# A two-normalisation, three-layer channel network on 16 images: one GELU over both token halves of the lower channels, shorter GroupNorm chains, and another instruction order

## What is computed

```python
x = x + had(gn(x))                      # gn: 32 groups of 6 channels; had: 192 x 192 Hadamard block
h = gn(x)                               # x: (16, 192, 56, 56)
h = gelu(layernorm(W1 h + b1) * g1 + beta1)     # over the 192 channels of each pixel
h = gelu(layernorm(W2 h + b2) * g2 + beta2)
x = x + W3 h + b3
```

## Time and profile before

| | us |
|---|---|
| median of 3 runs | 1047.11 |
| lowest and highest | 1045.45, 1048.05 |
| the profiled execution | 1043.52 |
| its span, first to last instruction | 1041.7 |

### The profile page before, as it was taken

The page is one execution under the profiler, slowest core; times in us unless marked ns, Lnnn a source line. Parts: engine busy times, 40 slices in busy tenths (PEclk is TensorE's granted clock), DMA queues, the critical chain, the costliest instruction groups (busy, mean ns, idle before and its releaser), DMA issues.

```text
span 1041.7 us, 25024 instructions
## 1 busy us (share of the span) xinstructions
PE 932.8 (90%) x9384; PEld 638.9 (61%) x9384; DVE 868.4 (83%) x1553; ACT 890.1 (85%) x2821; POOL 612.5 (59%) x477
## 2 busy tenths in 40 slices
PE   0637898999998999999998999999999999999995
PEld 0216565666666666666765666666676666677662
DVE  6798999998999899999899989999889877854542
ACT  0727887899988998899988998889998999899992
POOL 0533654566665667556665667566665666666662
PEclk9967999999999999999999999999999999999997
DMA  9524021132222222222322232222101111011111
GB/s 288 158 78 109 28 81 55 54 107 77 85 81 81 81 81 86 77 85 78 107 71 74 85 94 81 81 81 81 54 31 52 34 50 54 28 54 55 54 46 62
DMA packets 49080, 80.66 MB, mean 77 GB/s; under 512 B 5568, under 2 KB 48704, under 8 KB 48832
## 3 DMA queue, kind: packets, MB, share of 16 engines
q1 hardware_dynamic: 48960, 79.06, 24.8%
HBM read 40.51 MB, written 38.54 MB: 76 GB/s over the span
## 4 chain that ended last, share of the span: by engine, by line
PE 68%; DVE 22%; POOL 3%; ACT 2%; issue 2%; SPq 1%; DMA 1%; POOLq 0%; ACTq 0%; DVEq 0%
PE tm L415 18%; PE tp L427 9%; PE tm L409 8%; PE tm L402 5%; PE hl L351 5%; PE hl L315 4%; DVE z L871 3%; PE hl L373 3%; PE tp L433 3%; PE hl L356 3%; PE hl L368 3%; DVE X L745 3%; DVE bn L720 3%; DVE x_lo L861 2%; PE hl L320 2%; DVE xs_lo L736 2%
## 5 line engine op out<-in xcount | busy, mean ns | idle before, releaser
L626 POOL TENSOR_TENSOR ge_lo<-ge,ge_hi 128x672 f16<-128x672 f32 x224 | 334.5, 1494 | 131.4 <-ACT ge_hi L532 131.4
L617 POOL TENSOR_TENSOR rs<-ssq,neg_half 112x4 f32<-112x4 f32 x224 | 246.6, 1101 | 228.0 <-ACT z L503 228.0
L503 ACT ACTIVATE z<-tm 112x194 f32<-112x194 f32 x896 | 284.3, 340 | 29.0 <-PE tm L415 29.0
L871 DVE TENSOR_TENSOR z<-tm,rs 112x768 f32<-112x768 f32 x224 | 212.6, 949 | 55.7 <-POOL rs L617 54.2
L516 ACT ACTIVATE ge<-tp,par 128x448 f32<-128x448 f32 x224 | 163.6, 731 | 53.6 <-PE tp L427 45.6
L503 ACT ACTIVATION_READ_ACCUMULATOR z<-tm 112x1 f32 x896 | 194.9, 217 | 0.0
L532 ACT ACTIVATE ge_hi<-ge 128x672 f16<-128x672 f32 x224 | 174.4, 778 | 2.2
L427 PE MATMUL tp<-cst,z 112*128 112x112 f32 x896 | 134.9, 273 | 14.8 <-DVE z L871 13.0
L745 DVE SCALAR_TENSOR_TENSOR X<-hl,h_bias,X 128x448 f32<-128x448 f32 x161 | 105.0, 678 | 50.4 <-PE hl L320 42.3
L427 PEld LDWEIGHTS tp<-cst,z 112*128 112x128 f32 x896 | 89.5, 142 | 87.8 <-issue 59.6
L494 ACT ACTIVATE x_hi<-X,gscale 128x448 f16<-128x448 f32 x168 | 106.8, 671 | 21.2 <-DVE gscale L819 21.2
(11 more groups left out here) (138 smaller groups left out, 2181.5 us busy)
## 6 DMA issues: line engine op xcount, KB each, us to landing
X<-x SPq DMA_DIRECT2D x56, 448.0 KB, 3.7
out<-X SPq DMA_DIRECT2D x56, 448.0 KB, 2.7
X<-x SPq DMA_DIRECT2D x112, 112.0 KB, 3.7
out<-X SPq DMA_DIRECT2D x112, 112.0 KB, 2.8
X<-weights SPq DMA_DIRECT2D x1, 1024.0 KB, 12.2
cst<-consts SPq DMA_DIRECT2D x1, 704.0 KB, 9.7
X<-biases SPq DMA_DIRECT2D x1, 192.0 KB, 2.5
par<-params SPq DMA_DIRECT2D x1, 6.5 KB, 1.6
```

Source lines behind the costliest of these rows:

```text
L503: last = nc.scalar.activation(z[n][:, 2 * h + k, i * TW:(i + 1) * TW], tm[h][:, i, k * TW:(k + 1) * TW], ACT.Square, scale=float(C) ** -0. ...
L617: nc.gpsimd.tensor_tensor(rs[n][:, 2 * h:2 * h + 2, :], ssq[n][:, 2 * h:2 * h + 2, :], neg_half[0:TT, 0:4].rearrange("p (i k) -> p i k", i=2),
L626: nc.gpsimd.tensor_tensor(ge_lo[n][:, g % 2, :, cols], ge[n][:, :, cols], ge_hi[n][:, g % 2, :, cols], ALU.subtract).then_inc(s_ge_lo[n], 1)
L871: nc.vector.tensor_tensor(z[n][:, 2 * h:2 * h + 2, 0:2 * C].rearrange("p k (i o) -> p i k o", i=2), tm[h][:, :, 0:2 * TW].rearrange("p i ( ...
```

## The change

One: `gelu` of the lower channels. Both halves' transposes of the lower channels now go into the two halves of `tp`'s bank 1, and one ACT instruction of 448 columns, in the call for h = 1, takes both. The tiles `ge`, `ge_hi`, `ge_lo` are laid out anew: [upper h0 image 0, image 1, upper h1 image 0, image 1, lower h0, lower h1], each 224 columns; `gelu_hi` and `gelu_lo` take parts of 448 (h = 0) and 896 columns (h = 1) instead of 672 and 672. `group(g, 1, 0)` waits for both parts. The matmuls keep their number and sizes.

Two: small operations. `gn_shift` leaves out the factor -1 and writes both copies with one instruction (the sign moves to `gn_h_bias` and `gn_w1_bias`, which subtract); `gn_w1_bias` works on 128 partitions in three instructions instead of ten on 2-row slices; `layer_biases` likewise. In the prologue fewer `stats_x` blocks stand between the parts of the second GroupNorm (7 instead of 10, the rest goes to step 0), `gn_w1_bias(0)` stands before `x1_split_lo(0, b)`, and on POOL `groupnorm_rstd(0, 1)` stands behind the subtraction for `w3_lo`.

Three: the order of the calls in `step` on PE, ACT, DVE and POOL.

```diff
-FIRST_STATS = {0: (42, 42), 1: (42, 52), 2: (52, 56), 3: (56, 63)}
+FIRST_STATS = {0: (42, 42), 1: (42, 54), 2: (54, 54), 3: (54, 63)}
...
-                    pe.wait_ge(s_ge_lo[0], 2 * g + h + 1)
+                    pe.wait_ge(s_ge_lo[0], 2 * (g + 1))
...
             def step(g):
                 group(g, 0, 0)
+                transposes(g - 2, 1, 1)
                 h_ab(h_unit(g, 0))
-                transposes(g - 2, 1, 1)
                 group(g, 0, 1)
                 h_c(h_unit(g, 0))
                 gn_means(gn2_pair(g), 1)
+                group(g - 1, 1, 0)
                 gn_means(gn1_pair(g), 0)
                 transposes(g, 0, 0)
-                group(g - 1, 1, 0)
                 l3_ab(g - 2)
                 transposes(g, 0, 1)
+                group(g - 1, 1, 1)
                 w1_shift(gn2_pair(g))
-                group(g - 1, 1, 1)
...
-                nc.scalar.activation(ge[n][:, 2, cols], tp[:, 1, 0:HALF], ACT.Gelu,
-                                     bias=par[:, 4 * n + 3:4 * n + 4], scale=par[:, 4 * n + 1:4 * n + 2]).then_inc(s_ge[n], 1)
+                if h == 1:
+                    act.wait_ge(s_tp[n], 3 * (g + 1))
+                    nc.scalar.activation(ge[n][:, 4:6, :], tp[:, 1, 0:2 * HALF].rearrange("p (b t) -> p b t", b=2),
+                                         ACT.Gelu, bias=par[:, 4 * n + 3:4 * n + 4], scale=par[:, 4 * n + 1:4 * n + 2]
+                                         ).then_inc(s_ge[n], 1)
...
-            groupnorm_rstd(0, 1)
             pool.wait_ge(s_whi, 3)
             nc.gpsimd.tensor_tensor(w3_lo[:, :, :], w3st, w3_hi[:, :, :], ALU.subtract).then_inc(s_wlo, 1)
+            groupnorm_rstd(0, 1)
...
-                for rows in two:
-                    last = nc.vector.tensor_copy(bias_rows[0][rows, 0, 0:C], b_row[rows, :])
-                do(last)
-                for rows in two:
-                    last = nc.vector.scalar_tensor_tensor(out=b_row[rows, :], in0=bias_rows[0][rows, 0, 0:C],
-                                                          scalar=row1[rows, :], in1=b_row[rows, :],
-                                                          op0=ALU.mult, op1=ALU.subtract)
+                do(nc.vector.tensor_copy(b_hi[:, :], b_row[:, :]))
+                nc.vector.scalar_tensor_tensor(out=bias_rows[0][:, :, 0:C],
+                                               in0=b_hi[:, :].unsqueeze(1).to_broadcast([128, 2, C]), scalar=low_row,
+                                               in1=b_row[:, :].unsqueeze(1).to_broadcast([128, 2, C]),
+                                               op0=ALU.mult, op1=ALU.add).then_inc(s_bias, 1)
```

More of the change, by code:

```diff
@@ L27 @@
 BND = 6
+PART = (slice(0, 2), slice(2, 6))
 AA, CA_, AC_, CCB, CCD = range(5)
@@ L350, in l3_ab @@
                     for r, (w, act) in enumerate(terms):
-                        nc.tensor.matmul(hl[:, i, 0:UT], w[:, AA, :], act[:, i, :], start=(r == 0), stop=False,
+                        nc.tensor.matmul(dst[:, i], w[:, AA, :], act[:, i:4:2, :], start=(r == 0), stop=False,
                                          skip_group_check=True)
@@ L355, in l3_ab @@
                         rows = slice(64 * i, 64 * i + 64)
-                        last = nc.tensor.matmul(hl[:, i, 0:UT], w[rows, CA_, :], act[rows, 2, :], start=False,
+                        last = nc.tensor.matmul(dst[:, i], w[rows, CA_, :], act[rows, 4:6, :], start=False,
                                                 stop=(r == 2), skip_group_check=True)
@@ L367, in l3_c @@
                 for r, (w, act) in enumerate(terms):
-                    nc.tensor.matmul(hl[:, 0, 0:UT], w[:, CCB, :], act[:, 2, :], start=(r == 0), stop=False,
+                    nc.tensor.matmul(dst, w[:, CCB, :], act[:, 4:6, :], start=(r == 0), stop=False,
                                      skip_group_check=True)
@@ L372, in l3_c @@
                         cols = slice(64 * i, 64 * i + 64)
-                        last = nc.tensor.matmul(hl[cols, 0, 0:UT], w[:, AC_, cols], act[:, i, :], start=False,
+                        last = nc.tensor.matmul(dst[cols], w[:, AC_, cols], act[:, i:4:2, :], start=False,
                                                 stop=(r == 2), skip_group_check=True)
@@ L422, in transposes @@
                 pe.wait_ge(s_z[n], 2 * g + h + 1)
-                done = 4 * g + 2 * h
+                done = 3 * g + h
                 free("tp0")
@@ L729, in first_stats @@
                 if g == 0:
-                    stats_x(range(31, 42))
+                    stats_x(range(28, 42))
             def scaled_lo(a, b):
@@ L807, in gn_shift @@
                     return
[L808 removed]
                 dve.wait_ge(s_grs, gn_use(q, n) + 1)
                 scale = (gscale1[:, q % 2, :], gscale2[:, :])[n]
[L811 to L818 removed]
+                for rows, cols, w in ((slice(0, 128), slice(0, 2), 2), (lower[0], slice(2, 3), 1), (lower[1], slice(3, 4), 1)):
+                    if n == 0:
+                        nc.vector.tensor_tensor(gshift[0][rows, cols, 0], gmu[rows, 0, cols], scale[rows, cols], ALU.mult)
+                    else:
+                        shape = [rows.stop - rows.start, w, 2]
+                        nc.vector.scalar_tensor_tensor(out=gshift[1][rows, cols, :],
+                                                       in0=gmu[rows, 0, cols].unsqueeze(2).to_broadcast(shape),
+                                                       scalar=b3[rows, cols.start:cols.start + 1],
+                                                       in1=scale[rows, cols].unsqueeze(2).to_broadcast(shape),
+                                                       op0=ALU.add, op1=ALU.mult)
                 nc.vector.tensor_copy(scale[lower[1], 2:3], scale[lower[1], 3:4]).then_inc(s_gn[n], 1)
```

161 lines of the change are left out of this document (73 added, 88 removed).

## The result

The changed kernel takes 998.68 us (median of four runs, 997.27 to 999.54) against 1047.58 us of the kernel before on the same chip (four runs): a ratio of 0.9536, 95% interval 0.9516 to 0.9555. The profiled execution took 999.41 us, its span is 997.6 us; the span before was 1041.7.

The account below looks back on a forecast made before the run. It took PE, busy without a gap, to bound regular steps at 15.8 us. Terms -4.0 (prologue), -6.0 (steps 0 to 5), -18.5 (GroupNorm), -2.5 (end), +1.3 (tail) sum to -29.7: median 1047.1 to about 1017, range 1008 to 1037.

Parts of the forecast that it names:

- The two tight waits: Regular step: `group(g-1, 1, 0)` waits for `z(g, 0, 0)`, half a microsecond left, and for all of `ge_lo`, 4.7 us left.
- rivals A: Regular step: the half microsecond before layer 2's first half is eaten, 0.4 us in each of 42 steps, 1034; chance 0.15.
- D: Regular step: `ge_lo` holds DVE instructions 1.7 us beyond DVE's slack, 42 times, so slower, 1088; chance 0.10.
- The idle times of 1.49, 1.05 and 1.20: GroupNorm steps: PE's waits at `w1_shift`, the next `h_ab` (six steps each) and `l3_c` (four) go, 20.0 us together.
- the 1.5 kept back for ACT: GroupNorm steps: 20.0 cut to 18.5, as ACT's wait in `split_x1(g+1, 0)` can make transposes 0.2 to 0.4 late.
- 0.3 is left: GroupNorm steps: the bias ends at 17.1 us from the step's start, the next step starts at 17.4.
- it passes: GroupNorm steps: the last bias instruction starts 0.2 us behind an `rs` whose successor isn't ready, so it isn't held.
- Rival B: GroupNorm steps: bias caught behind `rs` and the 896-column `ge_lo`, 2.3 us in each of six steps, 1031; chance 0.10.
- All these read two operands from SBUF: DVE and POOL: such DVE instructions are held when `ge_lo` runs or waits behind `rs`, for the rest of both.
- the prologue's 4.0: Prologue gain: 1.1 stuck operation, 1.7 for three `stats_x`, 1.8 shorter bias, less 0.6 waiting for PE's means.
- I get 1.8 gained over steps 0 and 1: Steps 0 and 1: three blocks return (1.7), but `normalise` precedes the statistics and `GELU` isn't behind `scaled_hi`; 1.8 us gained.
- Rival C: Norm steps: DVE is next, PE's gaps reappear ahead of other blocks; only prologue and removed instructions count, 1030; chance 0.07.

Follow-up runs that it names:

- `h_ab` turned round: Kernel after, with the 64-row matmuls of `h_ab` first and those over 128 rows and 96 columns after them; 1008.7 us, ratio 0.9636.
- before, with one piece of PE's order: Kernel before, with `transposes(g-2, 1, 1)` moved ahead of `h_ab(h_unit(g, 0))` on PE, nothing else; 1080.86 us, ratio 1.0331.
- transposes ahead of `l3_c`: Kernel after, with `transposes(g - 1, 1, 0)` moved ahead of `l3_c(g - 2)` on PE; 1023.28 us, ratio 0.9773.

## Why the prediction was wrong, point by point

**The regular step, where it failed.** "PE bounds such a step without a gap; a step can't be shorter unless PE's work shrinks, and the change leaves every matmul as it is", and then "So I expect 15.8 again". I had set PE's blocks one behind the other with lengths taken beside their old neighbours, and a block's length belongs to the pair. Over five kernels, in regular steps without idle time (PE busy for all of each window):

| kernel | shape changes between blocks | regular step, us |
|---|---|---|
| before | 8 | 15.78 |
| `h_ab` turned round | 7 | 15.59 |
| before, with one piece of PE's order (step 47) | 6 | 15.50 |
| after | 5 | 15.35 |
| transposes ahead of `l3_c` | 4 | 15.20 |

Counted from the kernel after, each change is worth 0.12 to 0.15 us. Three of them, 0.43 a step, in 42 steps are 18 of the 21 us by which steps 6 to 47 beat the forecast. The trace of before could have told it: in its `l3_ab` matmuls of 448 columns start 0.19 us apart, and the 64-row pair behind them 0.29 after the last. `l3_ab` waits only at its head, so this tenth can't be a wait:

```profile
606.91 0.35 PE L351 MATMUL hl<-ge_lo,w_hi 128*128 128x448 f16 x1
607.10 0.35 PE L351 MATMUL hl<-ge_hi,w_lo 128*128 128x448 f16 x1
607.39 0.36 PE L356 MATMUL hl<-ge_hi,w_hi 64*128 64x448 f16 x2
```
The Trainium skill (TensorEngine Tiling (Array Packing), Key Properties) says that changing the tiling mode drains TensorE. The trace agrees, and puts 0.12 to 0.15 us to one change; I had not weighed that rule, though the change consists of moved blocks.

**The two tight waits of the regular step.** Right: no idle time in it, rivals A and D did not occur. The runs with only a part of the orders show how narrow it was, 0.2 to 1.4 us of waiting in each regular step.

**The GELU.** "I cost it at nothing by itself": in the regular step it measured 0.06 us, close. "It pays only where ACT was late": it does pay outside the regular steps, and I put no number to that. With the new orders the part is worth 13.8 us in all. That ACT is what is late there isn't shown; in step 27 of the run without it PE waits 0.54 us for a residual of DVE.

**GroupNorm steps.** Of 20.0 gross I took 18.5; 21.4 came. The idle times of 1.49, 1.05 and 1.20 are all gone, and the 1.5 kept back for ACT wasn't needed. (The 21.4 rest on taking 0.43 for each of the 42 steps.)

**The bias.** "0.3 is left" and "it passes" were right, by less than 0.2 us. Rival B was real in its mechanism and forecast too cheap: 2.3 us in each of six steps, where the run with the old small operations lost 6.5 in each of seven. I had left out that the clock is low behind a gap of 4 us. And "All these read two operands from SBUF" was too narrow: the cast was held too. The Trainium skill (SBUF — State Buffer, Who interferes with whom) counts casts and copies that go into a mode with two ports among those that exclude GpSimd; the 2.58 us of the cast agree. `x_lo` at 563.39 isn't alone: all eight `x_lo` of the kernel before that began inside an `rs` took 0.68 or 0.69, and the last bias operation of the kernel after took 0.62 wholly inside the `rs` from 535.55, as it does with no `rs` about (71.31). An `rs` alone held none of them. Why the `gshift` triple at 522.37, with a `ge_lo` right behind the `rs`, was held and `x_lo`, with one right behind as well, was not, remains unexplained.

**Prologue and steps 0 to 5.** -10.0 forecast, -4.2 measured. The terms of the second norm's chain held: PE's idle times ahead of `w1_shift` and of the first group went from 4.95 and 5.00 to 2.67 and 3.25, 4.0 together, and the bias in three operations took 1.3 (70.63 to 71.93). So the prologue's 4.0 was right. That the first group came only 3.0 earlier is the part ahead of this chain: the Hadamard stages ended at 58.7 instead of 57.7, and over all fifteen kernels run here that time lies anywhere from 56.3 to 59.8. The step that failed is "I get 1.8 gained over steps 0 and 1": they lost 2.2. Step 0 has 14 `stats_x` blocks in a row, 7.46 us, ahead of the means. I counted their time once (1.7 for three), and neither PE's wait for them nor the lower clock that goes with it. Steps 2 and 4 gained 1.1 and 1.3 instead of 1.6 each, steps 3 and 5 together 1.1 (1.0 forecast).

**End and tail.** 14.17 for 14.1, -2.3 for -2.5, +1.8 for +1.3: right. Of the tail's 1.8, 1.5 are PE's idle time ahead of `l3_ab`, which waits for the 896-column `ge_lo` (2.12 and 4.18 us instead of 1.46 and 3.38). That the sum came so close is in part luck: the GELU part alone costs the tail 2.9, and the rest of the change gives 1.1 back.

Rival C, that the order wouldn't do its work, was half right in an unexpected way. The small operations alone give 14 us in the old order, and undone in the new order they take 48 away. The parts don't add: GELU 14, small operations 48, PE's order 54 and the other orders 88, each taken away alone, sum to four times the gain.

## What to carry to other kernels

A full engine isn't a floor: where blocks that use the whole array alternate with 64-row or 64-column ones, count the places where the shape changes, and let neighbours share a shape. Take a block's length from a place with the same neighbours on both sides. Where DVE and POOL share SBUF, the price of a small operation on the critical path is whether it is over before POOL's next long one begins; shorten or move it by tenths, and look at every such place again after each change that shifts the step.

## What the runs showed of the hardware that I had not expected

- A change between full-array, 64-row and 64-column matmuls costs TensorE 0.12 to 0.15 us; with six transposes between two 64-row blocks 0.72 us instead of 0.58.
- A cast of 192 columns from fp32 to fp16 in SBUF took 2.58 us instead of 0.26 while POOL ran two subtractions of 1.89 and 1.04 us back to back. A hold outlasts the boundary of two POOL instructions.
- Behind an idle time of PE of 4.35 us the granted clock was 0.50 for the next 4.60 us. Behind one of 2.14 us, in the kernel with transposes ahead of `l3_c`, it was 0.50 from 0.5 us later on, and the step was 5.3 us longer. Behind the 1.80 us at 130.89 in the kernel before it stayed 1.00 up to 134.0.
